# A 127-row copy split into 112 and 15 rows, and a second buffer for the spread norms, in a two-part transformer kernel

## The reference, cut to what matters

```python
x = x + causal_attention(layernorm(x))          # 4 x 512 tokens, width 128, 16 heads of 64
y = layernorm(x)
for i in range(6):                              # DEPTH
    y = attn_layer(shift_tokens(y), ...) + y    # window attention
    y = ffn_layer(shift_tokens(y), ...) + y
x = x + y

def shift_tokens(t):                            # upper 64 channels from the token before
    a, s = split(t, 2, -1)
    return concat([a, pad(s, one token ahead)[:, :-1]], -1)

def attn_layer(x, Wqkv, qs, ksc, Wo):
    q, k, v = split(x @ Wqkv, 3)                # 16 heads of 64
    q, k = l2norm(q) * qs, l2norm(k) * ksc      # norm over the 64 channels of a head
    q, k = rotary(q) , rotary(k)                # with a scale that grows for q, shrinks for k
    return local_attention(q, k, v) @ Wo        # windows of 32, own window and the one before
```

## Time and profile before

| | us |
|---|---|
| median of 3 runs | 2067.93 (2065.5 to 2072.03) |
| the profiled execution | 2079.58 |
| its span in the profile | 2077.6 |
| PE busy | 1934.1 (93%) |
| DVE busy | 1495.4 (72%) |
| POOL busy | 1384.6 (67%) |
| ACT busy | 1213.9 (58%) |

### The profile page before, as it was taken

One profiled execution on the slowest core, in us unless ns is written; L12 is line 12 of the kernel. 1 busy time (PEld: TensorE's weight loads), 2 busy tenths in 40 slices (PEclk: granted clock), 3 DMA queues, 4 the chain that ended last, 5 costly groups with the idle time before them and its releaser, 6 DMA issues.

```text
span 2077.6 us, 71775 instructions
## 1 busy us (share of the span) xinstructions
PE 1934.1 (93%) x28614; PEld 1375.0 (66%) x28614; DVE 1495.4 (72%) x3441; ACT 1213.9 (58%) x2533; POOL 1384.6 (67%) x1360
## 2 busy tenths in 40 slices
PE   9999999998689999999999999999999999999977
PEld 5555555555466777777777777776777777777755
DVE  5666766665577787777787777787777787787753
ACT  5665666664345665656655666655666556665633
POOL 3334443433787787877697877788786797787741
PEclk9999999999789999999999999999999999999999
DMA  4000000000455566556546556456754557555440
GB/s 128 6 1 11 1 6 6 6 1 12 111 129 122 135 151 138 121 128 148 139 112 148 136 139 143 109 128 142 169 131 97 126 123 178 133 116 127 110 121 24
DMA packets 249455, 208.54 MB, mean 100 GB/s; under 512 B 72096, under 2 KB 239780, under 8 KB 248996
## 3 DMA queue, kind: packets, MB, share of 16 engines
q1 hardware_dynamic: 249124, 203.96, 42.1%
HBM read 84.19 MB, written 3.67 MB: 42 GB/s over the span
## 4 chain that ended last, share of the span: by engine, by line
PE 25%; SPq 23%; POOL 7%; issue 6%; DVE 6%; DMA 6%; ACT 3%; DVEq 0%; ACTq 0%; POOLq 0%
SPq L1014 9%; PE bank L1150 8%; DMA RB<-norms 5%; PE bank L1129 5%; PE bank L941 4%; POOL T L1021 4%; SPq L1036 3%; SPq L1007 3%; PE bank L1322 2%; PE bank L1298 2%; SPq L1038 2%; PE bank L1067 2%; SPq L117 2%; POOL T1F L1021 1%; DVE PL L1084 1%
## 5 line engine op out<-in xcount | busy, mean ns | idle before, releaser
L1021 POOL TENSOR_TENSOR T<-T,RB 128x512 f32<-128x512 f32 x304 | 378.3, 1279 | 161.0 <-DMA RB<-norms 160.8
L941 PE MATMUL bank<-XT,WQK 128*128 128x256 f32 x1520 | 385.3, 395 | 39.3 <-DVE T L960 35.9
L965 POOL TENSOR_TENSOR T<-T 128x512 f32<-128x512 f32 x304 | 387.0, 1280 | 31.9 <-DVE T L960 30.8
L1150 PE MATMUL bank<-WU,YS 128*128 128x128 f32 x3072 | 371.8, 279 | 34.6 <-ACT YS L1137 21.9
L1150 PEld LDWEIGHTS bank<-WU,YS 128*128 128x128 f32 x3072 | 356.6, 194 | 57.9 <-issue 53.0
L682 POOL TENSOR_SCALAR PR<-PR,RI 128x512 f32<-128x512 f32 x256 | 173.7, 693 | 300.4 <-DVE RI L571 299.1
L941 PEld LDWEIGHTS bank<-XT,WQK 128*128 128x128 f32 x1520 | 279.0, 194 | 131.7 <-DVE T L960 64.9
L959 DVE TENSOR_TENSOR T<-bank,TAB 128x512 f32<-128x512 f32 x304 | 208.4, 685 | 177.8 <-POOL T L965 135.4
L1137 ACT ACTIVATE YS<-bank 128x512 f32<-128x512 f32 x384 | 214.3, 602 | 181.3 <-PE bank L1129 180.2
L490 ACT ACTIVATE PR<-PR,NM 128x512 f32<-128x512 f32 x256 | 183.5, 717 | 165.2 <-DVE NM L566 164.2
L1105 POOL TENSOR_TENSOR PL<-PL,RIL 128x512 f32<-128x512 f32 x192 | 202.4, 1055 | 87.9 <-DVE RIL L1098 87.8
(11 more groups left out here) (146 smaller groups left out, 3016.7 us busy)
## 6 DMA issues: line engine op xcount, KB each, us to landing
RB<-norms SPq DMA_DIRECT2D x384, 128.0 KB
QP<-T SPq DMA_DIRECT2D x304, 128.0 KB
KZ<-T SPq DMA_DIRECT2D x304, 128.0 KB
TAB<-rotary_dram SPq DMA_DIRECT2D x24, 512.0 KB, 4.5
KZ<-T1F SPq DMA_DIRECT2D x80, 128.0 KB
QP<-T1F SPq DMA_DIRECT2D x80, 128.0 KB
WQK<-wqk_halves_dram SPq DMA_DIRECT2D x12, 512.0 KB, 5.8
norms<-RN SPq DMA_DIRECT2D x380, 4.0 KB
```

Of the source, the lines that this page charges most:

```text
L941: m = pe.matmul(b[:, ab * HALF:(ab + 1) * HALF], WQK[n % 3][:, i, ab, :], XT[s % 2][:, hf * HALF:(hf + 1) * HALF], start=True, stop=True)
L965: pool.tensor_tensor(t1, t1, T2[i % 2][:, ::-1, :], ALU.add).then_inc(l_rotated.sem, 1)
L1021: pool.tensor_tensor(t1, t1, RB[:, i:i + 1, :].to_broadcast([P, 2, HALF]), ALU.mult).then_inc(l_scaled.sem, 1)
L1150: m = pe.matmul(bank[7][:, 0:E], YS[:, h, :], WU[:, lp * HG + lane, i * E:(i + 1) * E], start=h == 0, stop=h == HEADS - 1)
```

## The change

Two edits. In `sp_keys` the transfer of 127 rows becomes two, of 112 and of 15 rows, so each step has four transfers on `s_keys` in place of three, and the waits on it count 64 in place of 48. And `RB` becomes two buffers of 128 x 4 x 256: front `f` uses `RB[f % 2]`, and `sp_norms_in(f)` waits for POOL's scaling of front `f - 2` in place of `f - 1`.

```diff
-            RB = sbl('RB', [P, HG, HALF])
+            RB = [sbl(f'RB{i}', [P, HG, HALF]) for i in range(2)]
...
             def sp_norms_in(f):
                 sp.wait_ge(s_rn, 64 * (f + 1))
-                sp.wait_ge(l_scaled.sem, l_scaled.at(f - 1))
+                sp.wait_ge(l_scaled.sem, l_scaled.at(f - 2))
                 rows = norms[f % 2].rearrange('(g h) (a c) -> h a g c', h=HG, a=1)
                 for h in range(HG):
-                    sp.dma_start(RB[h * WIN:(h + 1) * WIN, :, :], rows[h].to_broadcast([WIN, HG, HALF])).then_inc(s_rb, 16)
+                    sp.dma_start(RB[f % 2][h * WIN:(h + 1) * WIN, :, :], rows[h].to_broadcast([WIN, HG, HALF])).then_inc(s_rb, 16)
...
             def pool_scale(f, i):
...
-                pool.tensor_tensor(t1, t1, RB[:, i:i + 1, :].to_broadcast([P, 2, HALF]), ALU.mult).then_inc(l_scaled.sem, 1)
+                pool.tensor_tensor(t1, t1, RB[f % 2][:, i:i + 1, :].to_broadcast([P, 2, HALF]), ALU.mult).then_inc(l_scaled.sem, 1)
...
                 if t == 0:
-                    pe.wait_ge(s_keys, 48 * (s + 1))
+                    pe.wait_ge(s_keys, 64 * (s + 1))
...
-                sp.dma_start(o[1:P, :, DH:E], xb[0:P - 1, :, DH:E]).then_inc(s_keys, 16)
+                for r0, r1 in ((0, 112), (112, P - 1)):
+                    sp.dma_start(o[r0 + 1:r1 + 1, :, DH:E], xb[r0:r1, :, DH:E]).then_inc(s_keys, 16)
...
             def sp_back(s):
-                sp.wait_ge(s_keys, 48 * (s + 1))
+                sp.wait_ge(s_keys, 64 * (s + 1))
```

More of the change, by code:

```diff
@@ L1663, in sp_layers_program @@
                 sp.wait_ge(s_shift, 48 * STEPS)
-                sp.wait_ge(s_keys, 48 * STEPS)
+                sp.wait_ge(s_keys, 64 * STEPS)
                 sp.wait_ge(s_back, 32 * STEPS)
```

## The result

The kernel with both edits takes 2013.88 us (median of 4 runs, 2008.55 to 2018.64), against 2069.01 for the kernel before: a ratio of 0.9733 with a 95% interval of 0.9712 to 0.9753, 55 us less. The forecast was 2010. The profiled execution took 2018.64 us, where the forecast's sum gave 2021.6.

What follows compares the result with a forecast made beforehand. The prediction took SP's queue, stalled behind the 127-row copy, as the bound. Profiled 2079.58 - 58 (split) - 0 (second buffer) = 2021.6 us; profiled lies 11.65 above the median, so 2010 us, range 1992 to 2034.

Steps and rivals of the forecast that it cites:

- What bounds it: In SP's queue: the 127-row copy stalls the norms' spread behind it some 7 us; POOL, DVE and PE then wait.
- The cost of the split: One more issue a step on SP's queue: 0.9 us each, 21 us over the kernel, none on PE by itself.
- The term of 58.0 us: Stretches from `RN` of front 4s+2 to that of 4s+3: 23 x (17.56 - 15.04) us saved without the stall.
- PE's floor in the stretch to 4s+3: From `RN` of front 4s+2 to that of 4s+3, PE's work sets the length: 16.09 - 1.05 = 15.04 us.
- The 24th stretch: The stretch of this kind in the first step, not in the sum of 23 and left out of the forecast.
- The second buffer at nothing: SP's earlier spread from two `RB` buffers gains 0 at the end; upper bound 25.3 us of SP's waits.
- The three other stretches within 5 us: Sign of being right: sums of the other three kinds of stretch between two `RN` stay within 5 us.
- the 23 stretches near 346 us: Sign of being right: the stretches from `RN` of front 4s+2 to 4s+3 sum to near 346, from 403.90 us.
- Slower: Rival: the first spread still stalls after the split and starts 0.9 us later; 21 us lost, 2089 us; chance 0.03.
- Part of it: Rival: spreads or `RN` stay late, stretches to 4s+3 stop at 16.09 us; 33.8 us saved, 2034 us; chance 0.16.
- more: Rival: PE's waits for `RN` and for DVE's products all go, 71.3 us, in all stretches; 1997 us; chance 0.14.

## Why the prediction was right

*What bounds it.* Shown: the 127-row copy blocks SP's queue, the spread behind it is late, and POOL, DVE and PE lose in turn. The split alone brings the whole gain, the cuts show the stall growing with the rows of the badly spread piece, and the damage moves when the copy moves. The trace shows the first issue behind the copy held for 6.9 us, while the DMA engines are nearly idle. Whether a spread that was handed over in time would still land late behind the copy on the busy engine is less sure: the copy issued from ACT followed the spreads in most steps, and only four steps bear on it. That these rows go through exactly one engine stays a reading of the share of 0.09; no row names the engine. The Trainium skill (DMA: Bandwidth & Descriptors, Why a DMA increments its semaphore by 16 and not by 1) gives engine counts that fit all the cuts: 31, 61, 79, 97 and 127 have no divisor up to 16 but one, while 15 and 112 have 15 and 16. The share of 0.10 at 97 rows fits that too. One detail of the text ahead was wrong: the load of `WQK` stands behind the keys in the last step of each layer but the last (steps 3, 7, 11, 15 and 19), not in the first step of the next. These are five steps all the same, so no sum changes.

*The cost of the split.* Right: 1.61 us for the pair. That it lies off PE's path fits the 3.4 us of PE that are open in the stretches behind it, and SP's 69.3 us of waits for DVE.

*The term of 58.0 us.* It came out near the measured time, but in part by luck: the floor under it was wrong, and what was missed on either side cancelled. I took 15.04 us as PE's floor in the stretch to 4s+3; the 23 rows after have a mean of 14.28. That was no floor, because `RN` is DVE's event and can come before PE is through with its work. While DVE was late, PE had run its products L941 and L1298 before `RN` came, and so inside the window. With DVE on time a good part of them falls behind `RN`, into the next one: in step 9 `RN` begins at 1078.80, and PE runs L941 at 1077.34 and L1299 at 1079.16, where before `RN` came at 1110.07, after PE had ended both and begun to wait, at 1110.43 - 1.05 = 1109.38. PE's busy time shows it for all steps: 35.8 us less in the stretches to 4s+3, 23.9 more in those to 4s+4. So the first kind of stretch lost 75.5 us, the second gained 15.9 where no change was forecast, net 59.6 against 58.0. The two belong in one sum. The 24th stretch, which I left out, gave 6.2 us more, and the stretches to 4s+2 took 6.1 back. The profiled executions differ by 60.9 us and the medians by 55.1; the 58.0 was read from the one and taken off both.

```profile
1077.34 1.99 PE L941 MATMUL bank<-XT,WQK 128*128 128x256 f32 x8
1079.16 1.02 PE L1299 MATMUL bank<-XNT,W1S 128*114 128x512 f32 x2
```

*The second buffer at nothing.* Right, by both runs in which it stands alone or is taken away. A detail was wrong: I wrote that SP's wait would move to the relayout. It didn't: L1036 shows one wait of 1.5 us, L1038 none. The wait moved to the landing of the norms, 26.3 us before and 37.0 with both edits, as with the buffers alone.

*The remaining stall.* I had the four spreads at 1.75 us; they take 3.89 in step 9. This isn't the old stall in small. The first issue behind the copy is short, 0.49 us; the third takes 2.40, the longest of all. The second and the third in one row:

```profile
L1014 SPq DMA_DIRECT2D RB<-norms x2: 432/1415/2398, 1055.4 to 1055.9; - x2
```

In most steps one of the second to fourth spreads is held like this. The delay is no longer than the one behind 61 rows, which costs nothing. What it comes from wasn't tried.

*The three other stretches within 5 us.* Wrong for two of them, and the prediction had named a growing sum as a sign against it; it also had the 23 stretches near 346 us, and they are 328.4. One of the two was +15.9, explained above. The one to 4s+2 was +6.1: a few single rows carry it, above all this one, with a granted clock of 0.90. In the repeat of the same kernel the sum is 341.63, with the split alone 340.86, with 96 and 31 rows 338.97, and with the buffers alone 336.98, as before. So 2 to 6 us are lost there once the stall is gone; the cause stays open.

```profile
1169.70:1187.60 17.90, 15.41 (x272) 12.79 (x271) 12.44 (x31) 10.14 (x23) 13.51 (x15) 0.90 0.62 142
```

*The rivals.* "Slower" is what the rule for two halves in the Trainium skill (DMA: Bandwidth & Descriptors, Rules for kernel authors) would make of the split. It doesn't hold for this copy: the ratio is 0.9722 with the split alone, and the measurement decides. The rule has in view halves that each use all the engines, not a count of rows that spreads badly. "Part of it" and "more" ended 20 us above and 17 below the measured time. Of the 71.3 us of PE's waits that "more" gave up, 54.7 went (35.9 to 12.6 and 35.4 to 4.0).

## What to carry to other kernels

A DMA queue that only issues can be the longest link in the chain. Look for an issue that takes ten times its line's median, and blame the transfer ahead of it, not the one that waits. A copy shifted by one row has 127 of them; cut it so that the piece whose count spreads badly is short or, as with 112 and 15, there is none. Or issue it where nothing urgent stands behind it in the same queue, as the copy from ACT did. When a window ends at an event, work of other engines can change sides as the event moves, so add neighbouring windows before reading a gain off one of them.

## What the runs showed of the hardware that was not expected

The stall behind a badly spread copy grows evenly, 67 ns a row of four runs of 256 bytes from 61 to 97 rows. ACT's slow copy doesn't hold up SP's issues as SP's own does: the eight relayout issues around it in step 9 take 5.90 us against 6.04 with both edits, and the longest of all 384 takes 1.99 us, against 1.98 in the repeat of both edits. Behind SP's own 127-row copy the first issue takes 6.9. And a piece of 31 or 61 rows costs no more than the one of 15, within what the runs can tell (0.4% to either side).
